# An attention block with a gated network: the last chunk's first 12 heads projected earlier, and the first group's later loads issued later

## What is computed

```python
x = L0_attn_x                                   # 4 x 2048 x 256, fp32
xn = _layernorm(x, axis=-1)
# s: attention, 16 heads of 16, keys j >= queries i only, then the output projection
scores = jnp.where(j >= i, (q @ k.T) / 4, -inf);  attn = softmax(scores)
s = (attn @ v).reshape(B, S, H) @ w_out + b_out
# g: a network of +1/-1 weights (512 -> 1024 -> 1024 -> 256) on [xn, -xn], then silu
g = _silu(_L0_ffn_ref(xn, ...))
out = x + s * g
```

## Time and profile before

| what | value |
| --- | --- |
| median of 3 runs | 2318.76 us (2318.16 to 2321.8) |
| the profiled execution: time, and its span | 2317.55 us, 2315.8 us |
| PE busy | 2230.2 us (96%) |
| DVE, ACT, POOL busy | 1811.5 us (78%), 1580.9 us (68%), 915.3 us (40%) |
| PE's busy tenths in 40 slices | 7997999999999999999999999999999999999985 |
| chain that ended last | PE 84%, DMA 6%, DVE 4%, SP's queue 2% |

### The profile page before, as it was taken

The page is one execution under the profiler, slowest core; times in us unless marked ns, Lnnn a source line. Parts: engine busy times, 40 slices in busy tenths (PEclk is TensorE's granted clock), DMA queues, the critical chain, the costliest instruction groups (busy, mean ns, idle before and its releaser), DMA issues.

```text
span 2315.8 us, 60916 instructions
## 1 busy us (share of the span) xinstructions
PE 2230.2 (96%) x23760; PEld 1539.8 (66%) x23760; DVE 1811.5 (78%) x4516; ACT 1580.9 (68%) x3199; POOL 915.3 (40%) x1080
## 2 busy tenths in 40 slices
PE   7997999999999999999999999999999999999985
PEld 6786776666666666677666666666666666666652
DVE  7774787888888878788888878788888787888722
ACT  5662466777777777777777677677777776776662
POOL 1003534333433534344453445343443544354433
PEclk9998999999999999999999999999999999999997
DMA  8984111111111313131121223131322212132221
GB/s 299 359 317 167 39 29 40 43 50 46 47 49 35 94 40 87 48 86 51 51 83 45 81 59 83 41 90 43 83 55 53 83 44 84 50 83 69 81 92 58
DMA packets 157844, 193.31 MB, mean 83 GB/s; under 512 B 65276, under 2 KB 102076, under 8 KB 157560
## 3 DMA queue, kind: packets, MB, share of 16 engines
q1 hardware_dynamic: 156600, 189.41, 27.2%
q10 hardware_dynamic: 960, 0.00, 0.0%
HBM read 112.13 MB, written 76.14 MB: 81 GB/s over the span
## 4 chain that ended last, share of the span: by engine, by line
PE 84%; DMA 6%; DVE 4%; SPq 2%; issue 1%; ACT 1%; POOL 1%; POOLq 0%; ACTq 0%; DVEq 0%
PE b_ps L1406 25%; PE b_pv_ps L1372 22%; PE b_ps L1343 15%; PE b_ps L1353 12%; PE b_ps L1402 5%; DMA a_xs<-L_attn_x 4%; PE b_ps L1427 3%; DVE a_stats L397 1%; DVE a_qk_parts L435 1%; ACT b_u L1492 1%; DVE b_part_max L1518 1%; SPq L113 1%; PE b_ps L1360 1%; SPq L1186 0%; PE a_qk_ps L291 0%
## 5 line engine op out<-in xcount | busy, mean ns | idle before, releaser
L1461 ACT ACTIVATE b_probs<-b_ps 128x512 f32<-128x512 f32 (+3 forms) x2560 | 1258.4, 538 | 563.8 <-PE b_ps L1343 533.7
L1518 DVE TENSOR_REDUCE b_part_max<-b_ps 128x1 f32<-128x512 f32 x1536 | 972.4, 681 | 184.0 <-PE b_ps L1353 177.2
L1353 PE MATMUL b_ps<-k_kst,k_qst 48*128 48x512 f32 (+3 forms) x2560 | 896.3, 391 | 8.7 <-DMA k_kst<-qk_parts 3.4
L1343 PE MATMUL b_ps<-k_qst,k_kst 50*128 50x512 f32 (+3 forms) x2560 | 891.7, 389 | 11.7 <-DMA k_qst<-b_max_parts 11.1
L1343 PEld LDWEIGHTS b_ps<-k_qst,k_kst 50*128 50x128 f32 x2560 | 431.9, 185 | 323.7 <-DVE b_part_max L1518 115.8
L1515 DVE CUSTOM_DVE_ANT_0 b_ps<-b_ps,k_mask 128x512 f32<-128x512 f32 (+3 forms) x1024 | 483.5, 513 | 153.8 <-PE b_ps L1353 147.1
L1372 PE MATMUL b_pv_ps<-b_probs,k_vst 128*32 128x512 f32 (+3 forms) x5120 | 597.5, 541 | 0.5 <-POOL b_probs L1247 0.2
L1406 PE MATMUL b_ps<-b_u_hi,k_w 64*128 64x256 f32 x4096 | 590.0, 281 | 2.1 <-ACT b_u L1492 1.1
L1406 PE MATMUL b_ps<-b_u_lo,k_w 64*128 64x256 f32 x4096 | 588.5, 280 | 0.0
L1353 PEld LDWEIGHTS b_ps<-k_kst,k_qst 48*128 48x128 f32 x2560 | 432.9, 185 | 137.6 <-DVE b_part_max L1518 43.5
L1406 PEld LDWEIGHTS b_ps<-b_u_hi,k_w 64*128 64x128 f32 x4096 | 460.7, 187 | 20.2 <-ACT b_z L1483 4.2
(11 more groups left out here) (105 smaller groups left out, 1922.6 us busy)
## 6 DMA issues: line engine op xcount, KB each, us to landing
qk_parts<-a_qk_parts SPq DMA_DIRECT2D x64, 512.0 KB, 3.9
k_kst<-qk_parts SPq DMA_DIRECT2D x384, 64.0 KB, 2.3
k_qst<-qk_parts SPq DMA_DIRECT2D x384, 64.0 KB, 2.3
a_xs<-L_attn_x SPq DMA_DIRECT2D x16, 512.0 KB, 6.0
xn_T<-a_xT SPq DMA_DIRECT2D x16, 512.0 KB, 5.7
...
```

Source lines behind the costliest of these rows:

```text
L1343: pe.matmul(dst[:, 0:cols], keys, qst[rows, c, pair, 0:cols], start=True, stop=True).then_inc(s_ready, 1)
L1353: pe.matmul(dst[:, 0:CHUNK - k1], qst[rows, c, pair, i * P:(i + 1) * P], kst[rows, k_slot(kc, g % 2), pair, k1:CHUNK], start=True, stop=Tr ...
L1461: act.activation(probs[:, s % P_SLOTS, h, 0:cols], ps[:, banks[place, 0][0], 0:cols], ACT.Exp, scale=HD ** -0.5).then_inc(exp_done, 1)
L1518: dve.tensor_reduce(dst, src, AX_X, ALU.max).then_inc(ring_read, 1)
```

## The change

**Start.** The first group's q and k of chunks 1 and 0 and all its v (28 DMAs in 8 events) had the first place of the second stage in SP's list; their due step is now -LEAD + 3 and a bit, behind the first `negmax`. Due so, the loads of v of chunks 3 and 2 come first. A call in `made` also lets a transpose of maxima be placed between pieces of the network before the first scores; it moves nothing on PE there.

**End.** Chunk 12's first 12 heads get a combine of their own, `PARTIAL`, at `base` + 4, ahead of the other three: heads fetched, inverted, spread, scaled and projected; DVE adds the bias and keeps the result in the tile `partial` (the v tile v_in, whose last copy is done by then). The other three chunks are due at `base` + 12, 21 and 30. `GATE_PARTIAL` at `base` + 37 fetches gate and x for chunk 12 into tiles that the network used (sig, u, with waits for its last use, but none for the store of chunk 13) and POOL makes gate times partial plus x. After the last product with v only `last_sums` and `last_project` follow.

```diff
-COMBINE_LAST = (("fetch", 0), ("fetch_heads", 0), ("invert", 1), ("spread", 2), ("bias", 2), ("scale", 4))
+PARTIAL = (("fetch_heads", 0), ("invert", 1), ("spread", 2), ("scale", 4), ("project", 6))
+GATE_PARTIAL = (("fetch", 0), ("bias", 2))
...
-                at = min(at, -LEAD - 1)
+                at = -LEAD + 3 + (CPB - c) * 0.1
...
-    chunks += [(base - 14, NCHUNK - CPB - 1, COMBINE), (base + 9, NCHUNK - 1, COMBINE_LATE),
-               (base + 18, NCHUNK - 2, COMBINE_LATE), (base + 29, NCHUNK - 3, COMBINE_LATE),
-               (base + 38, NCHUNK - 4, COMBINE_LAST)]
+    chunks += [(base - 14, last - 1, COMBINE), (base + 4, last, PARTIAL), (base + 12, last + 3, COMBINE_LATE),
+               (base + 21, last + 2, COMBINE_LATE), (base + 30, last + 1, COMBINE_LATE), (base + 37, last, GATE_PARTIAL)]
...
-    out += [(TOTAL + PV_LAG, 1.5 + 0.1 * half, "project", len(chunks) - 1, chunks[-1][1], half) for half in range(2)]
...
+            if self.scores == 0 and self.turns:
+
+                self.end_span()
+                self.whole_array()
...
+                        sp.wait_ge(u_split, splits)
+                        sp.wait_ge(gate_done, PIECES)
+                        sp.wait_ge(gate_stored, (PIECES - 1) * DMA)
+                        sp.dma_start(last_gates[0], scratch.gate[i, :, 0:FPU, :]).then_inc(fetched, DMA)
+                        sp.dma_start(last_xs, tokens(x_t, i)).then_inc(fetched, DMA)
...
+                        if e == PARTIAL_HEADS + 1:
+
+                            sp.wait_ge(partial_done, 2)
...
+                        sp.wait_ge(y_ready, 2 * e)
...
+                        pool.wait_ge(partial_done, 2)
+                        at, tokens = partial[:, rows], last_xs[:, rows]
+                        pool.tensor_tensor(at, last_gates[half], at, ALU.mult).then_inc(gated, 1)
...
+                    if e == PARTIAL_HEADS:
+
+                        dve.wait_ge(v_placed, GROUPS * CPB)
+                        dve.tensor_tensor(partial[:, rows], src, bo[:].unsqueeze(1).to_broadcast([P, FPU, H]), ALU.add
+                                          ).then_inc(ring_read, 1)
+                        dve.wait_ge(ring_read, uses)
+                        dve.sem_inc(partial_done, 1)
+                        continue
...
+                    dve.wait_ge(bias_done, 2 * NCHUNK)
+                    dve.tensor_tensor(partial[:, rows], src, last_gates[half], ALU.mult).then_inc(last_gated, 1)
                     dve.wait_ge(last_gated, half + 1)
-                    dve.wait_ge(y_ready, 2 * NCHUNK)
-                    dve.tensor_tensor(xs[:, rows], xs[:, rows], last_gated_bias[:, rows], ALU.add).then_inc(y_ready, 1)
+                    dve.tensor_tensor(last_xs[:, rows], last_xs[:, rows], partial[:, rows], ALU.add).then_inc(y_ready, 1)
```

More of the change, by code:

```diff
@@ L587, in side_events @@
                     continue
-                at = min(at, -LEAD - 1)
+                at = -LEAD + 3 + (CPB - c) * 0.1
             out.append((n * STEPS + at, 3.5, what, n, c))
+    base = (GROUPS - 1) * STEPS
+    last = NCHUNK - CPB
     chunks = [(n * STEPS + 11, n - NG, COMBINE) for n in range(NG, GROUPS - 1)]
-    base = (GROUPS - 1) * STEPS
-    chunks += [(base - 14, NCHUNK - CPB - 1, COMBINE), (base + 9, NCHUNK - 1, COMBINE_LATE),
-               (base + 18, NCHUNK - 2, COMBINE_LATE), (base + 29, NCHUNK - 3, COMBINE_LATE),
-               (base + 38, NCHUNK - 4, COMBINE_LAST)]
-    for e, (t, i, stages) in enumerate(chunks):
+    chunks += [(base - 14, last - 1, COMBINE), (base + 4, last, PARTIAL), (base + 12, last + 3, COMBINE_LATE),
+               (base + 21, last + 2, COMBINE_LATE), (base + 30, last + 1, COMBINE_LATE), (base + 37, last, GATE_PARTIAL)]
+    tokens = heads = 0
+    for t, i, stages in chunks:
         for n, (what, gap) in enumerate(stages):
-            if what in ("bias", "scale", "project"):
+            e = heads if what in ("fetch_heads", "invert", "spread", "scale") else tokens
+            if what in ("bias", "scale"):
                 out += [(t + gap + half, 1.0 + 0.001 * n, what, e, i, half) for half in range(2)]
+            elif what == "project":
+                out += [(t + gap + half, 1.0 + 0.001 * n, what, tokens, heads, i, half) for half in range(2)]
+            elif what == "spread":
+                out.append((t + gap, 3.7 + 0.001 * n, what, tokens, heads, i))
             else:
                 out.append((t + gap, 3.7 + 0.001 * n, what, e, i))
+        tokens += stages is not PARTIAL
+        heads += stages is not GATE_PARTIAL
     out += [(base + 34, 3.9, "last_weights"), (TOTAL + PV_LAG, 1.0, "last_sums")]
-    out += [(TOTAL + PV_LAG, 1.5 + 0.1 * half, "project", len(chunks) - 1, chunks[-1][1], half) for half in range(2)]
     return out + [(TOTAL + PV_LAG, 2.0 + half, "last_project", half) for half in range(2)]
@@ L986, in attend_and_combine @@
     uses_of_network = network_uses()
+    splits = sum(F_BANKS for use in uses_of_network if use[0] != "L2")
     first_layer = {e[4]: e[1] for e in order if e[0] == "F" and e[5] == "L0" and e[9]}
@@ L1079, in chunk_of @@
             return CPB - 1 - c
-        def gated_of(e):
-            return gated_bias if e < NCHUNK - 1 else last_gated_bias
-        def gate_of(e, half):
-            return gt[:] if e == NCHUNK - 1 and half == 1 else gate[:, half * FPU:(half + 1) * FPU]
         def f_bank(use, n):
@@ L1173, in _ @@
                     e, i = arg
[L1174 removed]
+                    n = HEADS if e != PARTIAL_HEADS else LAST_HEADS
                     sp.wait_ge(inverted, e + 1)
@@ L1419, in _ @@
                 elif what == "project":
-                    e, i, half = arg
+                    _, e, i, half = arg
                     dst = claimed((place, 0)).rearrange("p (t h) -> p t h", h=H)
@@ L1548, in _ @@
                     e, i = arg
-                    rows = slice(0, P if e < NCHUNK - 1 else LAST_HEADS * P // HEADS)
+                    rows = slice(0, P if e != PARTIAL_HEADS else LAST_HEADS * P // HEADS)
                     dve.wait_ge(sums_fetched, (e + 1) * DMA)
```

69 lines of the change are left out of this document (37 added, 32 removed).

## The result

The changed kernel takes **2308.16 us** (median of 5 runs, 2303.45 to 2309.24) against 2318.76: ratio 0.9946, 95% interval 0.9932 to 0.9961. It is faster by 10.6 us, and I forecast 28.3 (2290.5, range 2283 to 2299). The direction was right, the size and the range were wrong. The profiled execution took 2308.26 us, its span is 2306.4, and PE is busy 2228.7 us of it (97%).

The account below looks back on a forecast made before the run. PE's own work bounds the kernel (84% of the span), with waits at the hand-over and the end. Start -12.3 and end -15.5 give -27.8 us on 2317.55: 2289.8, stated as a 2290.5 us median, range 2283 to 2299.

Parts of the forecast that it names:

- The start: At the hand-over between the stages: PE's wait of 9.65 us and 2.6 us of slow clock go, -12.3 us in all.
- Rival (b): At the hand-over: the start gives nothing, rows held or POOL's delay on v reaching PE; 2302 us, chance 0.07.
- the spare time: At the hand-over: first maxima's rows release PE at 196.4, PE comes there at 199.8, so 3.4 us to spare.
- In between, nothing that the change moves can gain: Between hand-over and end: the slices show PE below 90% only near the start, the hand-over and the last two.
- The end: Last group's combine, with chunk 12's first heads projected ahead: span ends at 2300.3 for 2315.8, -15.5 us, between -19 and -10.
- the tail: From the last product with v to the end of the span: 12.6 us.
- the two partial halves cost PE 2 x 1.99: At chunk 12's partial projection: PE's cost for its two halves, 1.99 us each.
- DVE's stop: At the partial combine's inversion: DVE waits 3 us for chunk 12's sums, costing PE +1.2 us, between 0 and +3.
- chunk 14's lap: From DVE's end to PE's start on chunk 14 (store, fetch, bias, spread, scale): 22.5 us, as before.
- c, "the partial combine hurts more": At the end: DVE's inversion holds the maxima and each lap starts later; 2297 to 2303 us, chance 0.12.
- chunk 13's lap: From its predecessor to chunk 13's first half: 23.5 us, where before took 25.2.
- the gate's products for chunk 12: POOL's four operations on chunk 12's gate and x end 1.8 us before DVE wants them: cost 0.

Follow-up runs that it names:

- e1: The kernel before with only the start's part of the change, its end as before: 2310.53 us, ratio 0.9956.
- e8: The kernel before with the change's start and COMBINE's inversion, spread, scale and projection one step later, its end as before: 2302.16 us, ratio 0.9925.
- e7: The kernel before with only COMBINE's inversion, spread, scale and projection one step later, neither part of the change: 2313.71 us, ratio 0.9971.
- e2: The changed kernel with the start's part undone, so only the end's part: 2321.67 us, ratio 1.0003.
- e6: The change with chunk 12's partial scales and chunk 15's scales ahead of POOL's casts, chunk 14's behind them: 2294.86 us, ratio 0.9880.
- e5: The change with chunk 12's two partial scales one step earlier, ahead of four POOL casts: 2301.93 us, ratio 0.9919.
- e3: The change with chunk 14's two scales one step later, behind POOL's casts: 2302.77 us, ratio 0.9912.

## Why the prediction was wrong

**The start: right.** The rows at 193.6, PE at 198.55 without a wait, 12.2 us for 12.3, and no delay from v or POOL. Rival (b) is out: e1 alone brings 10.2, and e8 against e7 11.6. None of the eleven traces with the new start has a wait for the first rows. Two sizes were kinder in before's trace than elsewhere: e2 and e7, with the old start, wait 8.49 and 8.72 us there, not 9.65, so against them the start brings about 1 us less. And the spare time was about 1 us by the forecast's own sum (193.57 + 2.85 + 1.2 = 197.6, PE at 198.55), not 3.4.

**"In between, nothing that the change moves can gain": right, but it hid that something could be lost.** It goes by the slices, where PE shows 90% or more, and gives the waits between no term. There stood 2.35, 2.39 and 3.44 us, and the lengths of the waits and of the half-clock stretches behind them change from execution to execution. In the profiled execution they ate 6 us of the start's lead; in the medians about 2 (10.2 of e1 against 12.3).

**The end: wrong.** From R, by the forecast's own terms against the change and e6:

| term | forecast | after | e6_pool |
| --- | --- | --- | --- |
| R to the start of chunk 15's pair | 59.4 | 65.7 | 58.9 |
| the pair | 4.0 | 3.7 | 3.7 |
| its end to chunk 14's pair | 23.9 | 29.5 | 25.9 |
| the pair | 4.9 | 5.5 | 5.4 |
| its end to chunk 13's first half | 24.9 | 25.2 | 26.4 |
| to the last product's end | 9.0 | 8.4 | 9.5 |
| the tail | 12.6 | 12.5 | 12.6 |
| sum | 138.7 | 150.5 | 142.3 |

Two terms failed. The first: "the two partial halves cost PE 2 x 1.99", with DVE's stop (+1.2) as the only wait. DVE's stop was 0.90 us and cost nothing that the rows show; but POOL kept the second scale 4.4 us behind casts and a mask, PE waited 3.12, and the halves took 4.33 and 2.58 us. e5 shows that it was this: 59.5 with the casts behind. The second: chunk 14's lap, which I copied from before's 22.5 us, where POOL does both scales in a row as soon as the spread is there. After, 3.8 us of casts stood between the scales (with 6.93 us of waiting for PE and some 6 us at 0.51 behind it), and e3 shows 25.7 without them. The last 1.8 us to the forecast's 23.9 are open, and so are the 1.5 us of chunk 13's lap in e6. I had a rival for the fault (c, "the partial combine hurts more", 2297 to 2303), with the wrong engine in it and a size that held half of the miss; its chance of 0.12 was too low.

The rest of the end stood: the tail, chunk 13's lap after the change, the gate's products for chunk 12 hidden on POOL. The end part is worth nothing by the medians (e2) and 3.7 us by the first pair of traces. The three executions with this same end took 150.5, 153.5 and 156.7 us from R, the two with the end of before 154.2 (before) and 155.7 (e1). Some of that spread is the half-clock stretches, whose lengths differ; the rest is not taken apart.
